# First attention: GpSimd subtracts the maxima in scalar form, sets the masked scores itself and makes the middle bf16 parts; the mask products behind the turns go; four load semaphores

## The reference

```
dot    = q @ k.T                                    # 512 x 512 for each row and head
scores = dot * dot / (|q|^2 + |k|^2 - 2 dot + 1e-6)
scores = scores + triu(ones, 1) * -1e9              # only earlier tokens and the token itself
attn   = softmax(scores)
out    = (attn @ v) @ w_out + b_out
```

## Time and profile before

| | |
|---|---|
| time, three runs | 2663.3, 2664.49 (median), 2668.45 us |
| the profiled execution | 2662.7 us, of which the span is 2660.9 us |
| PE, DVE, ACT, POOL busy, share of the span | 95%, 80%, 75%, 64% |
| first score unit on PE to last | 38.2 to 1290.9 us |
| second attention's units on PE | 1572.6 to 2330.7 us |

### The profile page before, as it was taken

The page is one execution under the profiler, slowest core; times in us unless marked ns, Lnnn a source line. Parts: engine busy times, 40 slices in busy tenths (PEclk is TensorE's granted clock), DMA queues, the critical chain, the costliest instruction groups (busy, mean ns, idle before and its releaser), DMA issues. The chain is left out here.

```text
span 2660.9 us, 73392 instructions
## 1 busy us (share of the span) xinstructions
PE 2514.8 (95%) x26276; PEld 1807.2 (68%) x26276; DVE 2135.9 (80%) x6793; ACT 2003.7 (75%) x3679; POOL 1693.0 (64%) x3088
## 2 busy tenths in 40 slices
PE   5999999999999999999879999999999999989998
PEld 3677777777777777777523336777777776768887
DVE  5999999999989999998674667888888888746665
ACT  4998999998899998998624447766676667657776
POOL 3767667667667767767451227777776777756555
PEclk8999999999999999999989999999999999999999
DMA  4334234334234434425100126566566556400001
GB/s 124 64 67 83 56 67 84 72 58 84 62 60 84 79 57 78 73 48 86 36 8 1 36 51 115 96 104 106 93 102 104 103 97 98 71 2 25 33 33 40
DMA packets 110378, 182.09 MB, mean 68 GB/s; under 512 B 27008, under 2 KB 96384, under 8 KB 97920
## 3 DMA queue, kind: packets, MB, share of 16 engines
q1 hardware_dynamic: 106176, 175.82, 35.5%
q10 hardware_dynamic: 3840, 1.58, 0.3%
HBM read 116.25 MB, written 60.29 MB: 66 GB/s over the span
## 5 line engine op out<-in xcount | busy, mean ns | idle before, releaser
L923 POOL TENSOR_TENSOR ratio_scores<-ratio_scores,ratio_max_cols 128x512 f32<-128x512 f32 (+3 forms) x1024 | 727.7, 728 | 318.3 <-DVE ratio_max_cols L808 312.5
L199 PE MATMUL bank<-ratio_k_stack,ratio_q_stack 102*128 102x512 bf16 (+7 forms) x2048 | 506.0, 303 | 33.6 <-DVE ratio_max_cols L808 17.5
L1483 DVE CUSTOM_DVE_ANT_0 zeroed_unused<-bank,zeroed_drop 128x512 bf16<-128x512 f32 (+3 forms) x1024 | 439.7, 484 | 107.3 <-PE bank L199 107.2
L808 DVE CUSTOM_DVE_ANT_0 ratio_scores<-bank,ratio_scores 128x512 f32<-128x512 f32 (+3 forms) x1024 | 472.5, 490 | 22.2
L1365 ACT ACTIVATE arena<-bank 128x512 f32<-128x512 f32 x640 | 370.3, 593 | 150.8 <-PE bank L1258 149.4
L657 ACT ACTIVATE ratio_prob<-bank 128x512 f32<-128x512 f32 x640 | 378.7, 592 | 104.9 <-PE bank L555 102.4
L798 DVE TENSOR_TENSOR ratio_scores<-bank,ratio_inverse 128x512 f32<-128x512 f32 x640 | 436.2, 682 | 16.8 <-PE bank L199 9.6
L552 PE MATMUL bank<-const_f_sb,ratio_scores 128*128 128x128 f32 x2560 | 410.0, 274 | 0.9 <-ACT ratio_prob L657 0.9
L646 ACT ACTIVATE ratio_inverse<-bank 128x512 f32<-128x512 f32 x640 | 381.1, 596 | 12.5 <-PE bank L202 12.5
L650 ACT ACTIVATE ratio_inverse<-ratio_inverse 128x1024 f32<-128x1024 f32 x320 | 338.7, 1058 | 10.1
L1617 POOL TENSOR_SCALAR_AFFINE_SELECT arena<-arena 128x256 f32<-128x256 f32 (+1 forms) x640 | 229.1, 364 | 163.7 <-ACT arena L1365 159.8
(11 more groups left out here) (219 smaller groups left out, 4973.6 us busy)
## 6 DMA issues: line engine op xcount, KB each, us to landing
ratio_q_stack<-ratio_parts_q SPq DMA_DIRECT2D x186, 128.0 KB
ratio_k_stack<-ratio_parts_k SPq DMA_DIRECT2D x186, 128.0 KB
zeroed_q_stack<-zeroed_parts_q SPq DMA_DIRECT2D x186, 128.0 KB, 4.4
zeroed_k_stack<-zeroed_parts_k SPq DMA_DIRECT2D x186, 128.0 KB, 7.5
ratio_parts_q<-arena SPq DMA_DIRECT2D x96, 128.0 KB
ratio_parts_k<-arena SPq DMA_DIRECT2D x96, 128.0 KB
zeroed_parts_q<-shared_parts SPq DMA_DIRECT2D x96, 128.0 KB
zeroed_parts_k<-shared_parts SPq DMA_DIRECT2D x96, 128.0 KB
```

The costliest lines, as they stand in the source:

```text
L199: i = e.matmul(bank[:, off:off + w], qs[0:rows, s, hh, ib * P:(ib + 1) * P], ks[0:rows, s, hh, 0:w], start=(k == 0), stop=mask is None, sk ...
L808: i = e.tensor_tensor_reduce(seg, dot_banks[n % 2][:, at], seg, 1.0, 0.0, ALU.mult, ALU.max, mx[:, pair % M_BUFS, c:c + 1])
L923: i = e.tensor_tensor(seg, seg, mx[:, pair % M_BUFS, c:c + 1].to_broadcast([P, w]), ALU.subtract)
L1483: i = e.tensor_tensor_reduce(unused[:, n % 2, at], bank[:, at], drop[:, L - (ib + 1) * P:L], 1.0, 0.0, ALU.add, ALU.max, mx[:, pair % FOLD ...
```

## The change

It does five things in the first attention.

1. `less(n)` on POOL becomes a `tensor_scalar`: score times -1.0 plus the maximum, which is read as one scalar for each partition. The result is maximum minus score, and the exponential on ACT gets `scale=-1.0`.
2. A new POOL step `drop_later(n)` behind it: one `affine_select` on the unit's diagonal blocks (one or two of 128x128) writes 1e30 where the column is later than the row. It waits for the new semaphore `below`, which `less(n)` raises; `lessened`, for which the turns wait, is now raised by `drop_later(n)`.
3. `turn(n)` on PE is four plain transposes. The 1024 products with the mask constant are gone.
4. The middle parts of q, k (L769) and norms (L778) move from DVE to POOL, as `tensor_scalar(x, 1.0, 0.0, mult, add)`, just ahead of the low parts.
5. The 16 load semaphores become 4, shared in turn by rows b, b+4, ...

```diff
@@ pe: turn(n)
-                first = True
-                for _, ib, off in UNITS[n % N_UNITS]:
-                    wd = (ib + 1) * P
-                    for jb in range(ib + 1):
-                        at = slice(off + jb * P, off + (jb + 1) * P)
-                        e.matmul(bank[:, at], scores[:, n % S_BUFS, at], net.ident,
-                                 is_transpose=True, start=first, stop=False, skip_group_check=True)
-                        first = False
-                    i = e.matmul(bank[:, off + wd - P:off + wd], net.ident_b, net.mask(B_SCORE),
-                                 start=False, stop=True, skip_group_check=True)
+                for at in range(0, width(UNITS[n % N_UNITS]), P):
+                    i = e.transpose(bank[:, at:at + P], scores[:, n % S_BUFS, at:at + P], net.ident)
                 i.then_inc(s["turned"])
@@ act: exponential(n)
-                e.activation(prob[:, n % PROB_BUFS, 0:wd], exp_banks[n % 2][:, 0:wd], ACT.Exp).then_inc(s["prob"])
+                e.activation(prob[:, n % PROB_BUFS, 0:wd], exp_banks[n % 2][:, 0:wd], ACT.Exp, scale=-1.0).then_inc(s["prob"])
@@ dve: split(half, side) and norm(half)
-                q.wait_ge(s["prep_read"], ratio_prep(half // 2, f"{sides[side]}{m}"))
-                q.wait_ge(s[f"parts_{sides[side]}"], 48 * half)
-                e.tensor_copy(parts[:, side, 1, :], rest[:, :]).then_inc(s["mid"])
...
-                e.tensor_copy(n_parts[:, 1, :], n_rest[:, :]).then_inc(s["norm_mid"])
@@ pool
             def split(half, side):
+                q.wait_ge(s["prep_read"], ratio_prep(half // 2, f"{sides[side]}{half % 2}"))
+                q.wait_ge(s[f"parts_{sides[side]}"], 48 * half)
+                e.tensor_scalar(parts[:, side, 1, :], rest[:, :], 1.0, 0.0, ALU.mult, ALU.add).then_inc(s["mid"])
                 q.wait_ge(s["mid"], 2 * half + side + 1)
                 e.tensor_tensor(parts[:, side, 2, :], rest[:, :], parts[:, side, 1, :], ALU.subtract).then_inc(s["lo"])
...
+                e.tensor_scalar(n_parts[:, 1, :], n_rest[:, :], 1.0, 0.0, ALU.mult, ALU.add).then_inc(s["norm_mid"])
...
-                    i = e.tensor_tensor(seg, seg, mx[:, pair % M_BUFS, c:c + 1].to_broadcast([P, w]), ALU.subtract)
-                i.then_inc(s["lessened"])
+                    i = e.tensor_scalar(seg, seg, -1.0, mx[:, pair % M_BUFS, c:c + 1], ALU.mult, ALU.add)
+                i.then_inc(s["below"])
+
+            def drop_later(n):
+                units = UNITS[n % N_UNITS]
+                blocks = scores[:, n % S_BUFS, :].rearrange("p (k t) -> p k t", k=T)
+                diagonal = blocks[:, 1::2, :] if len({ib for _, ib, _ in units}) < len(units) else blocks[:, T - len(units):T, :]
+                q.wait_ge(s["below"], n + 1)
+                e.affine_select(diagonal, diagonal, [[0, 2]][:len(units) - 1] + [[-1, P]], ALU.is_ge, dropped, 0, 1).then_inc(s["lessened"])
...
+            dropped = e.to_reg(-MASK_DROP)
...
                 if n < total:
                     less(n)
+                    drop_later(n)
@@ loads
+    def x_loaded(self, b):
+        return self.x_sems[b % X_SEMS], 16 * (b // X_SEMS + 1)
```

More of the change, by code:

```diff
@@ L46, in constants @@
     return f, b
+X_SEMS = 4
 class Seq:
@@ L263, in load_start @@
     nc = net.nc
-    net.x_loaded = [ctx.enter_context(nc.semaphore(f"x{b}_loaded")) for b in range(net.B)]
+    net.x_sems = [ctx.enter_context(nc.semaphore(f"x{i}_loaded")) for i in range(X_SEMS)]
     s = semaphores(nc, ctx, "start", "const_b const_f")
@@ L270, in _ @@
             row = lambda b: x_dram[b].rearrange("(t p) d -> p t d", p=P)
-            e.dma_start(net.xb(0), row(0)).then_inc(net.x_loaded[0], 16)
+            e.dma_start(net.xb(0), row(0)).then_inc(net.x_sems[0], 16)
             e.dma_start(stage[:, :], cb_dram).then_inc(s["const_b"], 16)
@@ L274, in _ @@
             weights.load(q)
-            e.dma_start(net.xb(1), row(1)).then_inc(net.x_loaded[1], 16)
+            e.dma_start(net.xb(1), row(1)).then_inc(net.x_sems[1], 16)
         @block.vector
@@ L289 @@
     norm_hi norm_mid norm_lo parts_q parts_k norms_q norms_k gathered_first gathered0 gathered1 q_ones k_ones v_ones
-    denoms log_den inverse dots weighed maxima lessened post_filled post_read
+    denoms log_den inverse dots weighed maxima below lessened post_filled post_read
     turned prob attended o_group rec_den x_bias"""
@@ L750, in normal @@
             def normal(b, pair):
-                q.wait_ge(net.x_loaded[b], 16)
+                q.wait_ge(*net.x_loaded(b))
                 q.wait_ge(s["rstd"], b + 1)
@@ L774, in norm @@
                 e.tensor_tensor(n_rest[:, :], prepared(half // 2, f"n{half % 2}")[0:64, :], n_parts[:, 0, :], ALU.subtract).then_inc(s["prep_read"])
-                q.wait_ge(s["prep_read"], ratio_prep(half // 2, f"n{half % 2}"))
-                q.wait_ge(s["norms_q"], 16 * half)
-                q.wait_ge(s["norms_k"], 16 * half)
-                e.tensor_copy(n_parts[:, 1, :], n_rest[:, :]).then_inc(s["norm_mid"])
             def values(half, pair):
@@ L912, in norm @@
             def norm(half):
+                q.wait_ge(s["prep_read"], ratio_prep(half // 2, f"n{half % 2}"))
+                q.wait_ge(s["norms_q"], 16 * half)
+                q.wait_ge(s["norms_k"], 16 * half)
+                e.tensor_scalar(n_parts[:, 1, :], n_rest[:, :], 1.0, 0.0, ALU.mult, ALU.add).then_inc(s["norm_mid"])
                 q.wait_ge(s["norm_mid"], half + 1)
@@ L991, in sp @@
                 if m and b + 2 < B:
-                    e.dma_start(net.xb(b + 2), x_dram[b + 2].rearrange("(t p) d -> p t d", p=P)).then_inc(net.x_loaded[b + 2], 16)
+                    e.dma_start(net.xb(b + 2), x_dram[b + 2].rearrange("(t p) d -> p t d", p=P)).then_inc(net.x_sems[(b + 2) % X_SEMS], 16)
                 sem = gathered(half)[0]
```

## The result

The changed kernel took 2638.88 us in the median of four runs (2632.14 to 2642.4) against 2665.69 for the kernel before on the same chip. The ratio is 0.9895, with a 95% interval of 0.9873 to 0.9916. Run once more unaltered, beside later experiments, it took 2632.32 us against 2663.94: 0.9885 [0.9866, 0.9905]. So it is faster by 28 to 31 us, clear of noise, inside the range of 2588 to 2660 and above the likeliest 2622.

A forecast was written before the change was run, and what follows sets the result against it. In the first attention PE, DVE and ACT are nearly full and no one is always the bound; DVE leads from slot 2 for some eight slots. Terms -48 - 6 + 8 + 3 + 1 = -42 give about 2622 us, range 2588 to 2660.

The forecast's parts named there:

- POOL's price: Scalar subtraction on POOL in the first attention: 178 ns + 0.91 ns per column, taken from affine_select's rows.
- the sum said 30.7: POOL's work per half of the first attention: 30.7 us forecast against 27.5 before, fitting at 81% of about 38.
- Rival 1: POOL becomes the bound in the first attention: 2.6 ns per column gives about 3040 us, 4.0 some 3570; chance 0.13.
- DVE loses two casts and one norm cast: Casts leaving DVE in the first attention: 1.56 us per half over 31 halves, -48 us, bounds 0 and 48.
- all of it lies in the stretch where DVE leads: Step of the cast term: the 1.56 us per half lie where DVE leads, from slot 2 for some eight slots.
- PE loses 1024 mask products: Mask products leaving PE in the first attention: some 60 us of PE's time, -6 us taken, bounds 0 and -60.
- rival 3: PE's relief counts too: ACT's 80.6 us waits for the turned bank shrink; 2580 to 2600 us, chance 0.07.
- The gather: Low parts leave POOL later, so PE waits about 1 us in each short half: +8 us, bounds 0 and +30.
- I take half: Half of the about 1 us gather wait per short half counted as time: 0.5 x 16 = +8 us.
- At nearly the same place: Reading that other short halves issue the last gather nearly where one did, at 735.57, with PE waiting 1.14 us.
- The port: DVE's normalization slows beside a busier POOL: 0.05 x 62 = +3 us, bounds 0 and +34.
- The start: The chain ahead of the first unit gets the longer middle parts: +1 us.

## Why the prediction was right, and where its terms were not

- **POOL's price, the number that was to decide, was right.** Forecast 178 ns + 0.91 per column, measured 269 + 0.83. The middle part takes 617 ns (forecast 640), the selects 406 and 292 as read from the earlier trace rows. POOL's work in a half is 32.0 and 29.1 us, mean 30.6, where the sum said 30.7. Rival 1, at 2.6 or 4.0 ns per column, did not happen. The Trainium skill (GPSIMD Engine Reference, sections 3.1 and 7) gives 1.03 cycles per element for a body of at most two operations, an estimated 0.86 ns at the 1.2 GHz that the page states. The trace agrees with its 0.83 for multiply and add, and does not for subtract and multiply, 4.0 ns. The choice of 0.91 rested on the likeness to the select; why the two slow rows are slow is still open.
- **"DVE loses two casts and one norm cast": mis-sized.** The term was -48 us (1.56 us in each half, all on the path). Alone the casts give 1.06 us per pair, 16 us; beside the masks 1.22, 19 us. The step that failed is "all of it lies in the stretch where DVE leads", and it failed in the rows of before: DVE did not run without a gap behind q's split, as was read. It stood for ACT ahead of k's split (758.55, 0.58 us) and in the short halves ahead of the norms (0.20 us in the mean). Of the 1.56 us, 1.15 became longer waits for ACT's square, ACT's norms and PE's dots. A cast that stands ahead of such a wait is worth nothing until the wait is shorter. The lower bound of 0 was named for that reason and then set aside because ACT had 2.7 us idle; idle somewhere in the half is not idle at the place.
- **"PE loses 1024 mask products": mis-sized the other way.** The term was -6 us, from DVE's own wait for PE. Measured alone 1.24 us per pair, 19 us, of the 60 that PE was relieved of. The 80.6 us that ACT waited for PE were the better row, and rival 3 had used it. With the masks gone and the casts still on DVE that wait fell to 73.0; in the changed kernel it is 63.7. Rival 3, which takes the whole gain from PE and ACT, was too high; its own terms give 2584 to 2608 us, not 2580 to 2600.
- **The gather: right in kind and size.** Forecast +8 us, measured 36.92 - 36.25 = 0.67 us per short half, 10 us. "I take half" was wrong as a law (the first 0.48 us are free, the rest counts in full). That the low parts leave POOL later was the small part of it: in the short halves the norms' leaves 8.89 us behind q's send and not 8.63, while PE asks 1.4 us earlier, and moving the splits on POOL changed nothing. "At nearly the same place" was a loose reading too: in the short halves before, the last gather is issued 15.8 to 17.6 us behind q's send, and the one of the earlier trace rows, at 17.3, is among the latest.
- **The port: nothing.** Forecast +3 us; DVE's normalization took 563 ns in the mean after, 610 before, in the same stretch, and its score products (`weigh`) 680 ns, 681 before.
- **The start: right as far as it can be told.** Forecast +1; q's parts of the second half left at 50.62 us and in the second run of the changed kernel at 49.89, before at 49.17.

The sum from these: 2.46 us x 15 pairs = -37, +10 for the waits, -27. The stage's 30 intervals behind the second send took 1153.7 us against 1180.6, which is -27.0. With +1.5 for the start, -25.5 of the profiled -30.5 are told. Of the other 5 us, some 2.4 lie in the last halves, up to the last score unit. The rest, 2.6, lies behind it in stages that the change does not touch. They take 1367 to 1376 us in the runs here, the longer the lower the granted clock is there: 1366.7 us at 0.99 in the changed kernel's second run, 1376.1 at 0.97 in the one with the copies. So 2 or 3 of the 28 to 31 us are not shown to be the change's.

In the terms of the sum the forecast of -42 had two errors of +29 and -13 that nearly halved each other. That they had opposite signs is luck. That it is faster and inside the range was earned by POOL's price and the gather, and would have held with either error alone; the middle was not earned.

## What to carry to other kernels

Where three engines are each over 90% busy and hand work to each other every 2 us, a microsecond taken from one of them was worth a fifth to six tenths of itself, whichever it was: 1.56 us of DVE gave 0.3 to 0.7, 1.9 us of PE 0.5 to 0.7, and 1.1 us added to ACT cost 0.4 to 0.7. Price each by the waits of all its neighbours, and look for the next wait of the same engine behind the place, however short: what is taken away ahead of it makes that wait longer first. Two reliefs together gave slightly more than their sum here, 2.46 against 2.30 us. And look at what has no slack beside the engines: the transfer that was just in time became, once the loop was 2% faster, a wait in every second half.

## What the runs showed of the hardware that was not expected

POOL's tensor_scalar is not one price. Multiply and add with one scalar column takes 0.83 ns per column (692 ns for 512), a comparison 2.6 (5449 ns for 2048), and subtract and multiply with two scalar columns about 4.0 (1231 ns for 256). Which property of the last two makes them slow was not tried.

One short half took 39.20 us, 1.4 more than its wait explains by the others. PE stood 1.98 us for the gather in it, the longest wait of the run, and the granted clock fell behind it (columns as in the earlier trace rows):

```profile
258.00:264.20 6.20, 4.15 (x59) 3.15 (x57) 6.06 (x24) 5.88 (x10) 4.02 (x10) 1.00 0.95 135
264.20:267.00 2.80, 2.80 (x38) 1.97 (x39) 1.94 (x8) 0.60 (x1) 2.11 (x5) 0.60 0.06 18
267.00:270.00 3.00, 3.00 (x33) 2.25 (x32) 2.13 (x6) 2.14 (x4) 1.34 (x3) 0.81 0.01 3
270.00:273.00 3.00, 3.00 (x29) 2.62 (x28) 2.91 (x9) 2.97 (x7) 2.02 (x4) 1.00 0.00 0
```

1.00 until PE was released at 264.2, then the 1.2 GHz level (0.50) from about 264.7 to 268.1, and 1.00 again. The waits of up to 1.74 us in the same run left no such mark: those halves have the length that the rule above gives.

The length of the wait does not decide it. The first row below is from the kernel with the added copies, where such a stretch began when PE had stood 1.89 us for ACT. The second is a short half of the kernel with the two-input subtraction, with a gather wait of 2.87 us in it and the clock at 1.00 throughout:

```profile
200.20:203.60 3.40, 3.40 (x4) 1.30 (x5) 0.47 (x2) 1.96 (x3) 0.98 (x2) 0.50 0.01 2
...
1020.93:1059.56 38.63, 33.80 (x374) 24.58 (x373) 33.08 (x104) 34.46 (x60) 34.47 (x59) 1.00 0.45 79
```

The half of the second row takes 38.63 us, which is 35.76 plus its wait and nothing more, and so it is with three others of that run, with waits of 2.02, 2.05 and 2.37 us; one with 2.54 fell. In the kernel with the early preparation and the late square the same wait of 2.1 us for the square stands in each of the 15 short halves, and the clock fell behind it in ten. Every fall from the second half to 1260 us, in all kernels here, began within 2.3 us of the end of a PE wait of 1.4 to 2.6 us and lasted 3.4 us; where the same half can be compared without one, it cost 1.1 to 1.7 us. So a wait of some 2 us can cost nearly twice what it shows, in some halves and not in others; what decides between them was not tested.
